# Gathering adjacency entries for 127 partitions in place of 128, with the last partition's flags zeroed beforehand

## What is computed

```
x = _layernorm(x + _L0_gnn_ref(x, adj, pairs, Wq, bq, Wk, bk), axis=-1)
x = _layernorm(x + _L1_gnn_ref(x, adj, adj), axis=-1)

# L0: softmax over the neighbours; only listed pairs that are edges have a score of their own
scores = jnp.zeros((HEADS, n, n)).at[:, sub, obj].set(att)       # sub, obj = pairs[:, 0], pairs[:, 1]
scores = jnp.where(mask[None], -jnp.inf, scores)                 # mask: no edge in adj
scores = scores.at[:, di, di].set(1e-07)
aggregator_factor = softmax(scores, axis=2).sum(axis=0) / HEADS
return aggregator_factor @ inst_feature
# L1: y = Coefficient2 @ (dinv * (sym(A) + I) * dinv) @ x, with adj for both matrices
```

## Time and profile before

| | us |
|---|---|
| three runs | 297.64, 300.83, 371.82 |
| their median | 300.83 |
| profiled execution, time | 298.47 |
| profiled execution, span from first to last instruction | 296.5 |

### The profile page before, as it was taken

One profiled execution on the slowest core, in us unless ns is written; L12 is line 12 of the kernel. 1 busy time (PEld: TensorE's weight loads), 2 busy tenths in 40 slices (PEclk: granted clock), 3 DMA queues, 4 the chain that ended last, 5 costly groups with the idle time before them and its releaser, 6 DMA issues.

```text
span 296.5 us, 3030 instructions
## 1 busy us (share of the span) xinstructions
PE 200.3 (68%) x887; PEld 86.3 (29%) x887; DVE 140.1 (47%) x357; ACT 86.4 (29%) x134; POOL 86.9 (29%) x100
## 2 busy tenths in 40 slices
PE   0069222121222127999999996989989799999991
PEld 0023000000000001444444442644434344444440
DVE  6987556410000000069928679264654444459532
ACT  4066565000000000077844441022121322116322
POOL 5777777777777710000000010043001000000000
PEclk9999655555555555899999999599999999999998
DMA  5999996500000000000996310027000830003211
GB/s 201 347 370 366 298 396 244 148 1 0 0 0 0 0 0 0 0 0 0 278 326 250 128 57 0 2 70 262 0 3 36 261 116 0 2 1 138 109 71 56
DMA packets 15757, 33.65 MB, mean 113 GB/s; under 512 B 3896, under 2 KB 4022, under 8 KB 15742
## 3 DMA queue, kind: packets, MB, share of 16 engines
q1 hardware_dynamic: 12526, 30.73, 30.3%
q0 software_dynamic: 3216, 2.74, 3.4%
HBM read 24.87 MB, written 8.60 MB: 113 GB/s over the span
## 4 chain that ended last, share of the span: by engine, by line
PE 63%; issue 28%; DVE 5%; ACT 1%; POOL 1%; DVEq 1%; POOLq 0%
PE ps L729 32%; PE ps L693 10%; PE ps L705 8%; PE ps L761 7%; PE ps L818 2%; DVE work L1167 2%; PE ps L778 1%; PE ps L934 1%; PE ps L807 1%; ACT xs L682 1%; DVE m_new L1307 0%; PE ps L908 0%; PE ps L812 0%; DVE rank L1161 0%; DVE rank L1162 0%
## 5 line engine op out<-in xcount | busy, mean ns | idle before, releaser
L729 PE MATMUL ps<-terms,at 128*128 (+1 forms) x242 | 69.7, 430 | 68.8 <-issue 68.4
L489 POOL DMA_INDIRECT kept<-in_adj_t,at_idx x79 | 76.8, 972 | 25.4 <-issue 23.8
L729 PEld LDWEIGHTS ps<-terms,at 128*128 (+1 forms) x242 | 24.8, 103 | 113.5 <-issue 92.0
L1107 DVE SCALAR_TENSOR_TENSOR xs<-xs,ratio,u 128x512 f32<-128x512 f32 x11 | 7.6, 748 | 63.1 <-ACT u L584 63.1
L761 PE MATMUL ps<-terms,bm 128*128 128x512 f16 x132 | 31.4, 394 | 0.0
L584 ACT ACTIVATE u<-ps,scale 128x512 f32<-128x512 f32 x11 | 6.6, 695 | 82.3 <-PE ps L729 82.3
L693 PE MATMUL ps<-terms,at 128*128 128x512 f16 x132 | 30.0, 379 | 0.9 <-DVE terms L1527 0.9
L729 PE MATMUL ps<-terms,bm 128*128 (+1 forms) x110 | 23.9, 379 | 0.0
L705 PE MATMUL ps<-terms,at 128*128 128x512 f16 x110 | 23.9, 379 | 0.0
L493 POOL IOTA xs<- 128x1408 f16 x1 | 1.3, 1300 | 68.1 <-DMA x_rows<-xs 68.1
L693 PEld LDWEIGHTS ps<-terms,at 128*128 128x128 f16 x132 | 12.8, 98 | 16.7 <-DVE terms L1527 1.4
(11 more groups left out here) (218 smaller groups left out, 222.5 us busy)
## 6 DMA issues: line engine op xcount, KB each, us to landing
work<-in_adj SPq DMA_DIRECT2D x6, 677.0 KB
bm<-in_adj_t SPq DMA_DIRECT2D x5, 677.0 KB
u<-in_adj_t SPq DMA_DIRECT2D x4, 677.0 KB
stage<-in_adj SPq DMA_DIRECT2D x4, 677.0 KB
u_rows<-u SPq DMA_DIRECT2D x10, 257.5 KB
x_rows<-xs SPq DMA_DIRECT2D x10, 256.0 KB
xs<-x_rows SPq DMA_DIRECT2D x10, 256.0 KB
out<-xs SPq DMA_DIRECT2D x10, 256.0 KB
```

Source lines behind the costliest of these rows:

```text
L489: pool.indirect_dma_start(out=kept[:, c:c + 1], out_offset=None, in_=adj_flat, in_offset=bass.IndirectOffsetOnAxis(ap=at_idx[:, c:c + 1], ...
L729: m = pe.matmul(ps[:, bank_of(i), :], matrix[:, bass.ds(k, 1), i * P:(i + 1) * P].rearrange("p o n -> p (o n)"), terms[:, s, bass.ds(k, 1) ...
L1107: dve.scalar_tensor_tensor(xs[:, i, :], xs[:, i, :], ratio[:, i:i + 1], u[:, i, 0:H], ALU.mult, ALU.add).then_inc(v_step, 1)
```

## The change

Each of the 79 gathers names partitions 0 to 126 of `at_idx` and `kept` in place of all 128. Partition 127 of `kept` is then written by nobody, so DVE zeroes `kept` once, as its second instruction, and POOL waits for that through a new semaphore before its first gather.

```diff
+LISTED = EFULL + 1
...
+        kept_clear = sem("kept_clear")
...
+            pool.wait_ge(kept_clear, 1)
             pool.wait_ge(idx_ready, 1)
             for (lo, hi), landed_in in zip(KEPT, kept_in):
                 for c in range(lo, hi):
-                    pool.indirect_dma_start(out=kept[:, c:c + 1], out_offset=None, in_=adj_flat,
-                                            in_offset=bass.IndirectOffsetOnAxis(ap=at_idx[:, c:c + 1], axis=0)).then_inc(landed_in, 16)
+                    pool.indirect_dma_start(out=kept[0:LISTED, c:c + 1], out_offset=None, in_=adj_flat,
+                                            in_offset=bass.IndirectOffsetOnAxis(ap=at_idx[0:LISTED, c:c + 1], axis=0)).then_inc(landed_in, 16)
...
             dve.memset(raw[:, :, :], N).then_inc(pads, 1)
+            dve.memset(kept[:, :], 0.0).then_inc(kept_clear, 1)
             dve.memset(xs[:, C - 1, :], 0.0).then_inc(pads, 1)
```

## The result

The changed kernel takes 392.2 us (median of 4 runs, 389.5 to 393.8) where the kernel before takes 299.5 us (median of 4): a ratio of 1.308, 95% interval 1.300 to 1.315; the ratio leaves out the one execution of the kernel before that took 371.82 us. The profiled execution took 392.62 us, its span is 390.5 us. The forecast of 299.1 us was wrong; of its rivals the first, slower by way of POOL, is what happened. The time lies between the 294 and 400 us of the range only because that range had been stretched into this rival.

What follows compares the result with a forecast made beforehand. It took PE's start, burst, 83 us slow stretch and about 180 us of dense work as the bound, the gathers bounding nothing. 298.47 + 0.1 + 0 + 0 = 298.6 us; on the near runs' mean 299.1 us, range 294 to 400 us.

Steps and rivals of the forecast that it cites:

- the first, slower by way of POOL: POOL from 4.5 us on: gathers over one queue are slow to write out; 376 us at 3.0 us per gather; chance 0.28.
- What bounds the kernel: Whole kernel: start, burst, 83 us of slow PE, then about 180 us of dense PE work; the gathers bound nothing.
- the valley: PE from 29.79 to 113.0 us: only 32 matmuls in 83.2 us at a clock of 0.51; the change was to leave it.
- The memset: DVE's start: zeroing `kept` takes 0.12 us and costs 0.1 us through x's load; the wait for `kept_clear` costs nothing.
- Price (b): POOL writing out the transfers of each gather: extra time near 0, in any case under 1.07 us per gather.
- d: Extra POOL time per gather, taken near 0; up to 1.07 us free, every further 0.1 us costing 7.9 us.
- the upper bound of 14.1: Largest extra POOL time per gather, if all 0.947 us went with one queue's elements: a gather of 15.0 us.
- 84.8 us of slack: Delay the last gather could take free: 79.6 us before DVE's read of block 6, plus 5.2 us at PE.
- the 5.2 us that were to be free behind PE's eight matmuls: PE's L770 takes DVE's total at 192.25 us, ready at 187.0 us, behind eight matmuls of L761.
- Price (a): DMA engines moving the gathers' data: 0.38 us of one engine per gather; cost taken as 0, at most 1.7 us.
- The valley hangs on the gathers: PE's slow stretch: gathers hold PE down, so no slack; 323 us at 0.3 us extra per gather; chance 0.05.
- The valley is gone: PE's slow stretch is shorter or gone by itself, untouched by the change: 225 us; chance 0.05.

## Why the prediction was wrong, step by step

**What bounds the kernel.** That the gathers bound nothing was right as to their data: nobody waits for them. It was wrong as to PE. The prediction took the valley as a given and said that no step of the change touches it. Without gathers it is gone (0.736), it moves when they move, and it ends soon after they end.

**The memset.** Right: `kept`'s memset took 0.12 us, the wait for the pairs fell from 0.27 to 0.20 us, and x's first load was still issued at 1.93 us. The wait for `kept_clear` was not free, though: with both waits POOL's first gather starts 1.1 us after `at_idx` was written (5.34 against 4.22 us) and with the memset alone 0.9 us (5.12 against 4.18); with one wait it is 0.3 us (4.50 before, 4.60 with the wait out). That is 0.6 to 0.8 us. On chips with the valley it should be hidden in the slack, but memset and wait with gathers of 128 were not run there.

**Price (b), POOL's writing: the step that failed.** The prediction put "the nearest row to a gather of 127 is the gather of 128 itself" and so d near 0. Measured, a gather takes 2.55 us, 1.60 more, and the pauses, for which the prediction had no term, add 0.6: d = 3.47 - 1.28 = 2.19 us, twice the 1.07 us that were free. The row of 128 priced only counts that are dealt out like 128. The argument that it is the same for 4 bytes or a row per partition spoke of bytes, not of how elements are divided; the prediction's own "for it" of the rival (with 16 queues the same step may serve 16 elements) came nearer, though the writing grew by 1.60 us and not by the upper bound of 14.1.

By the prediction's sum for that rival, with d and this run's own numbers: 78 x 2.19 = 170.8, less the 84.8 us of slack, plus 0.8 for the later first gather (5.3 against 4.5), plus 2.8 for a landing of 5.5 in place of 2.7 us, plus 4.2, because of the 5.2 us that were to be free behind PE's eight matmuls only 1.0 came back (the tail of 109.1 against 110.1). That is 93.8 us; the span grew by 94.0. Without the 47.2 us of pauses the same sum gives 46.6 us: about half of the loss hangs on the pauses, since the longer writing had by itself used up the slack. The rival's arithmetic held, and only its example (3.0 us per gather, 376 us) was a little short of the 0.95 + 2.19 = 3.14 us that a gather came to with the pauses.

**Price (a), moving the data.** 0.38 us of one engine per gather was too low by nearly sixty times: 48 packets of 455 ns are 22 us of engine time per gather. With it the early loads are slower (232 GB/s in the first window, 365 before; the first matmul of the long product starts at 18.34 in place of 17.49 us) and a landing takes 5.5 us. These two are small or hidden. The pauses are not small. They are longer while the loads run (6.3 to 7.9 us) than when the gathers are alone (3.5 us), which points to the moving of the data, but this is argued and not shown; whether POOL then waits for room among its unfinished transfers was not tried.

The Trainium skill, "DMA: Bandwidth & Descriptors", section "Why a DMA increments its semaphore by 16 and not by 1", says that the largest number of engines up to 16 that divides the partition count is used. POOL's own time follows this divisor for indirect gathers: 0.98 us at 126 and 120, 1.19 at 125, 1.28 at 124, 1.66 at 122, 2.53 at 127. The exception that it makes for some direct copies does not show in these gathers. Which engines moved the data was not read.

**The rivals.** "The valley hangs on the gathers" was right in its mechanism where there is a valley and wrong in its sum: it reckoned that a longer stream makes a longer valley, but the same number of gathers at a slower rate makes none. The prediction's argument against it, that ten gathers ran beside PE at full speed, fails because the slow-down comes only after some 20. "The valley is gone" came true too, and gave PE some 65 us, which went into waiting for the gathers, since the end was no longer set by PE. Without the valley, the gathers of 127 have no 84.8 us of slack. On the chip where the kernel before takes 220.6 us the changed kernel wasn't run; as its end hangs on the gathers alone, it should take about 390 us there too, 1.77 times as long; this is an estimate.

**The chances.** The rule was in hand, and so was the 15 us bound. To weigh a row that doesn't show the disputed quantity (a division by k) above both was the mistake.

## What to carry to other kernels

Keep the number of partitions of an indirect DMA a multiple of 16, or at least one with a large divisor up to 16, and fill unused slots with a harmless index: one element less made each gather 2.7 times as long. A row of the same operation at another count is no price for it; measure the count. And a slow stretch that the profile puts down to "issue" may belong to another engine's stream of transfers that nobody waits for: take the stream out once before calling the stretch a given. Look also whether other engines are late in it, at instructions that wait only for their own engine.

## What the runs showed of the hardware

On three chips of four, a stream of gathers of 128 elements, one per 1.25 us, brings PE down to one matmul per 2 to 3 us at half the clock after 20 to 28 gathers, holds up steps of DVE (by 3.4 and 4.5 us) and of ACT as well, and ends 4 to 11 us after the last gather. At one gather per 1.67 us or more in the mean there is no such stretch, only ripples in one of the runs, and at 1.55 us there are pieces of one. On the fourth chip the same stream (1.35 us in the mean with the memset alone) does nothing of the kind; whether that is the chip or the session is not known. DMA engines are not full in it (share 0.30 over the valley, 1.9% from 75 us on the earlier trace rows), and nobody waits for the gathers. The low clock alone does not explain it: in the burst 44 matmuls took 11.72 us, 0.27 us each, and twice that, an estimate for half the clock, is far from 2 to 3 us; and DVE is held up at instructions that wait for nothing of PE. What joins POOL's stream to the other engines is open. The single 371.82 us run of the kernel before stays unexplained too.
